# Finishing node batches inside the last six step groups of both graph convolutions

## The reference, cut to what matters

```python
def _gcn_layer(x, row, col, ew, W, b, n):
    deg = jax.ops.segment_sum(ew, col, num_segments=n)
    dis = jnp.where(deg > 0, jax.lax.rsqrt(jnp.maximum(deg, 1e-12)), 0.0)
    norm = dis[row] * ew * dis[col]
    h = x @ W
    msg = h[row] * norm[:, None]
    return jax.ops.segment_sum(msg, col, num_segments=n) + b
h = jax.nn.relu(_gcn_layer(x, row, col, ew, W1, b1, n))
out = _gcn_layer(h, row, col, ew, W2, b2, n)
x = _layernorm(x + out)
```

## Time and profile before

| | |
|---|---|
| median of three runs | 5566.82 us |
| lowest, highest | 5562.68, 5574.01 us |
| the profiled execution's own time | 5561.47 us |
| its span, first to last instruction | 5559.7 us |
| mean granted TensorE clock | 0.623 of full |
| GpSimd busy | 3855.6 us (69%) |
| VectorE busy | 3268.2 us (59%) |
| TensorE matmuls busy | 3136.6 us (56%) |
| ScalarE busy | 1490.0 us (27%) |

### The profile page before, as it was taken

One profiled execution on the slowest core, in us unless ns is written; L12 is line 12 of the kernel. 1 busy time (PEld: TensorE's weight loads), 2 busy tenths in 40 slices (PEclk: granted clock), 3 DMA queues, 4 the chain that ended last, 5 costly groups with the idle time before them and its releaser, 6 DMA issues. The chain is left out here.

```text
span 5559.7 us, 93044 instructions
## 1 busy us (share of the span) xinstructions
PE 3136.6 (56%) x16921; PEld 2725.2 (49%) x16922; DVE 3268.2 (59%) x11491; ACT 1490.0 (27%) x5614; POOL 3855.6 (69%) x4022
## 2 busy tenths in 40 slices
PE   4444444356666666679898989444444454444443
PEld 3333333345655555567777777333333343333332
DVE  6877777666777777754444444544444434444445
ACT  2333344336555555442222222300000010000001
POOL 3777777745777777637777775477777747777774
PEclk7555555568788788775555556655555565655555
DMA  5222222214444444312222221222222122222222
GB/s 124 54 53 53 53 53 57 47 46 127 131 131 131 131 131 131 101 44 58 53 54 53 57 53 30 56 55 55 54 53 53 52 59 55 55 55 54 53 53 58
DMA packets 229013, 386.29 MB, mean 69 GB/s; under 512 B 88799, under 2 KB 129084, under 8 KB 228688
## 3 DMA queue, kind: packets, MB, share of 16 engines
q0 software_dynamic: 141920, 294.25, 20.8%
q1 hardware_dynamic: 82924, 87.72, 5.3%
q10 hardware_dynamic: 3840, 0.99, 0.1%
HBM read 356.11 MB, written 26.56 MB: 69 GB/s over the span
## 5 line engine op out<-in xcount | busy, mean ns | idle before, releaser
L2298 POOL DMA_INDIRECT arena<-table_gcn,idx_now x1536 | 1457.9, 949 | 620.3 <-issue 418.8
L2393 PE MATMUL pair<-arena,hotf 128*128 x3328 | 752.9, 418 | 1111.9 <-POOLq L1881 1040.8
L2393 PEld LDWEIGHTS pair<-arena,hotf 128*128 128x128 f32 x3328 | 702.5, 320 | 1154.8 <-issue 1154.8
L2410 DVE TENSOR_SCALAR hotf<-iota,rel_now,ew_now 128x128 f32<-128x128 f32 x1664 | 444.1, 366 | 1000.7 <-PE pair L2396 925.9
L725 POOL DMA_INDIRECT arena<-table_attention,idx_now x832 | 813.0, 977 | 273.2 <-issue 208.1
L725 POOL DMA_INDIRECT arena<-table_key_value,idx_now x832 | 787.8, 947 | 276.0 <-issue 220.6
L1916 POOL DMA_INDIRECT arena<-table_edge_mlp,idx_now x784 | 754.1, 962 | 261.2 <-issue 210.9
L1132 PE MATMUL pair<-wide,hotf 128*128 128x130 f32 x1664 | 427.2, 436 | 645.2 <-ACT wide L1096 645.2
L1132 PEld LDWEIGHTS pair<-wide,hotf 128*128 128x128 f32 x1664 | 365.4, 323 | 709.7 <-ACT wide L1096 709.7
L2331 ACT COPY idx_now<-src_t 128x8 int32<-128x8 int32 x192 | 35.9, 197 | 1571.4 <-PE pair L2396 1209.7
L1468 PE MATMUL pair<-wide,hotf 128*128 128x132 f32 x1664 | 315.0, 348 | 232.8 <-DVE acc L1498 232.7
(11 more groups left out here) (384 smaller groups left out, 5666.3 us busy)
## 6 DMA issues: line engine op xcount, KB each, us to landing
arena<-table_gcn SPq DMA_DIRECT2D x1920, 0.5 KB
arena<-table_gcn ACTq DMA_DIRECT2D x1920, 0.5 KB
key<-rel_dram SPq DMA_DIRECT2D x104, 256.0 KB, 3.5
arena<-rel_dram SPq DMA_DIRECT2D x52, 512.0 KB
arena<-table_gcn,idx_now POOLq DMA_INDIRECT x1536
arena<-table_attention,idx_now POOLq DMA_INDIRECT x832, 2.5
arena<-table_key_value,idx_now POOLq DMA_INDIRECT x832, 2.9
arena<-table_edge_mlp,idx_now POOLq DMA_INDIRECT x784
```

The lines of the kernel that those rows point to most:

```text
L2298: q_.indirect_dma_start(conv_ring[:, slot * D:(slot + 1) * D], None, table, bass.IndirectOffsetOnAxis(ap=idx_now[:, slot:slot + 1].bitcast ...
L2393: t_.matmul(window[:, bass.ds(offset * D, D)], hot8[:, g % 2, u, :], conv_ring[:, bass.ds(slot * D, D)], start=False, stop=False)
L2410: last = v.tensor_scalar(out=hot8[:, g % 2, u, :], in0=iota[:, :], scalar1=rel_now[:, at], scalar2=ew_now[:, at], op0=ALU.is_equal, op1=AL ...
```

## The change

`convolution` gets four new arguments: what each engine does for settled batches. `SETTLED` is 98. Group k can only add to node tiles from 8k - 781 on, so once group 98 + j is added, batches 2j and 2j + 1 get no more sums. Behind each of groups 98 to 103 the engines run part j = k - 98 of the node work, and part 6 (batch 12) after the loop. Stages n4 and n5 as blocks of their own are gone.

In convolution one TensorE takes part too. From group 98 on it uses two sum windows instead of three (`pair[k % 2]`), and waits for one more clearing; the banks of `pair[2]` and `pair[3]` serve the node work, with one bank for `turn` and one for `hidden` instead of two each. The batches' temporaries move from `arena` and `hotf` into the unused `tab`.

```diff
+        SETTLED = -(-(ET - 1) // CG)
+        def convolution(name, table, table_out, settled_dve, settled_act, settled_sp, settled_pe=None, also_act=None, also_dve=None):
+            two_from = SETTLED if settled_pe else CSTEP_GROUPS
+            def window(k, g):
+                return pair[k % 2] if isinstance(k, int) and k >= two_from else pair[g % 3]
...
                         sp.sem_inc(sp_tile_in, 1)
+                    settled_sp(sp)
...
                         if k + AHEAD <= LONE * LONE_EVERY:
                             quarter(k + AHEAD)
+                        if k >= SETTLED:
+                            settled_act(act, k - SETTLED)
+                    for k in range(CSTEP_GROUPS - RING, CSTEP_GROUPS + 1):
+                        settled_act(act, k - SETTLED)
...
-                        pe.wait_ge(cleared, k + 1)
+                        pe.wait_ge(cleared, k + 2 if isinstance(k, int) and k >= two_from else k + 1)
...
                         last.then_inc(summed, 1)
+                        if settled_pe and isinstance(k, int) and k >= SETTLED:
+                            settled_pe(pe, k - SETTLED)
                     conv_rounds(pe, step, CSTEP_GROUPS)
+                    if settled_pe:
+                        settled_pe(pe, CSTEP_GROUPS - SETTLED)
...
-                        if not isinstance(k, int) or k + 3 < CSTEP_GROUPS:
+                        if not isinstance(k, int) or k + (3 if two_from > SETTLED else 2) < CSTEP_GROUPS:
...
                         back(k, g)
+                        if isinstance(k, int) and k >= SETTLED:
+                            dve.wait_ge(added, k + 1)
+                            settled_dve(dve, k - SETTLED)
...
                     conv_rounds(dve, both, CSTEP_GROUPS)
+                    settled_dve(dve, CSTEP_GROUPS - SETTLED)
```

More of the change, by code:

```diff
@@ new lines, in n4_pe, with turn, hidden, second @@
+        def n4_pe(pe, j):
+            def turn(b):
+                pe.wait_ge(n4_r, b + 1)
+                if b:
+                    pe.wait_ge(n4_rT_kept, b)
+                for u in range(BT):
+                    last = t_.transpose(turn_bank[:, u * P:(u + 1) * P], n4R[b % 4][:, u, :], ident[:, :])
+                last.then_inc(n4_rT, 1)
+            def hidden(b):
+                pe.wait_ge(n4_rT_kept, b + 1)
+                if b:
+                    pe.wait_ge(n4_h_kept, b)
+                t_.matmul(hidden_bank, wg1[:, :], n4T[b % 2], start=True, stop=True).then_inc(n4_h_mm, 1)
+            def second(b):
+                pe.wait_ge(n4_h_kept, b + 1)
+                if b >= 2:
+                    pe.wait_ge(n4_kept, b - 1)
+                for u in range(BT):
+                    at = slice(u * P, (u + 1) * P)
+                    last = t_.matmul(out_bank[b % 2][:, at], n4H[b % 2][:, at], wg2[:, :], start=True, stop=True)
+                last.then_inc(n4_mm, 1)
+            if j:
[7 more added lines that the diff above has]
+            hidden(2 * j)
+            if 2 * j + 1 == NB:
+                second(2 * j)
@@ new lines, in build, with n5_dve, sums, scales @@
+        n5_ch = Chain(v, n5_v)
+        def n5_dve(dve, j):
+            ch = n5_ch
+            def sums(b):
+                for t in range(b * BT, (b + 1) * BT):
+                    ch(v.scalar_tensor_tensor(out=xs[:, t, :], in0=acc[:, t, 0:D], scalar=dis[:, t:t + 1], in1=xs[:, t, :],
+                                              op0=ALU.mult, op1=ALU.add))
+                ch.wait()
+                for u in range(BT):
+                    ch(v.bn_stats(out=stat[:, u, 0:6], in_=xs[:, b * BT + u, :]))
+                ch.wait()
+                for u in range(BT):
+                    last = v.bn_aggr(out=n5M[b % 2][:, u, :], in_=stat[:, u, 0:6])
+                last.then_inc(n5_var, 1)
+            def scales(b):
+                f = n5F[b % 2]
+                dve.wait_ge(n5_std, b + 1)
+                ch(v.reciprocal(f[:, :, 0], f[:, :, 0]))
+                ch.wait()
+                v.scalar_tensor_tensor(out=f[:, :, 1], in0=n5M[b % 2][:, :, 0], scalar=-1.0, in1=f[:, :, 0],
+                                       op0=ALU.mult, op1=ALU.mult).then_inc(n5_factors, 1)
+            for b in (2 * j - 2, 2 * j - 1):
+                if b >= 0:
+                    scales(b)
+            for b in (2 * j, 2 * j + 1):
+                if b < NB:
+                    sums(b)
+            if 2 * j + 1 == NB:
+                scales(2 * j)
@@ new lines, in n5_act, with normalized, std @@
+        def n5_act(act, j):
+            def normalized(b):
+                act.wait_ge(n5_factors, b + 1)
+                for u in range(BT):
+                    t = b * BT + u
+                    last = s_.activation(xs[:, t, :], xs[:, t, :], ACT.Identity, scale=n5F[b % 2][:, u, 0:1], bias=n5F[b % 2][:, u, 1:2])
+                last.then_inc(n5_done, 1)
+            def std(b):
+                act.wait_ge(n5_var, b + 1)
+                if b >= 2:
+                    act.wait_ge(n5_done, b - 1)
+                s_.activation(n5F[b % 2][:, :, 0], n5M[b % 2][:, :, 1], ACT.Sqrt, bias=eps[:, 0:1]).then_inc(n5_std, 1)
+            for b in (2 * j - 2, 2 * j - 1):
+                if b >= 0:
+                    normalized(b)
+            for b in (2 * j, 2 * j + 1):
+                if b < NB:
+                    std(b)
+            if 2 * j + 1 == NB:
+                normalized(2 * j)
```

185 lines of the change are left out of this document (55 added, 130 removed).

## The result

The changed kernel's median was 5537.0 us (4 runs, 5527.95 to 5538.67) against 5569.7 us for the kernel before (4 runs): ratio 0.9939, 95% interval 0.9922 to 0.9956. Timed twice more, on other occasions, the ratio was 0.9966 (0.9952 to 0.9979) and 0.9953 (0.9940 to 0.9965). By medians that is a gain of 32.7, 21.2 and 26.5 us; the means of all 32 timings of before and 14 of the changed kernel are 25.7 us apart.

What follows compares the result with a forecast made beforehand. GpSimd's gathers were taken to pace the last groups, with about 72 us of n4 and n5 behind the convolutions. Gains of 21.2 (convolution two) and 3.4 (convolution one) make 24.6: 5566.82 to 5542.2 us, range 5532 to 5558.

Steps and rivals of the forecast that it cites:

- The step: Convolution two and n5: node work behind each group on VectorE and ScalarE; gain 21.7 us, 21.2 after output writes.
- the allowance: Convolution two: 13 output writes beside gathers might delay group 102; nothing to about 1 us, taken as 0.5.
- It fits, barely: Convolution two: VectorE's group work plus a part takes 9.8 us in a period of 10.05, so no backlog forms.
- The chain behind close 102: Convolution two: VectorE is the path from group 102's sum at 5515.32 to the last `normalized` ending at 5535.3.
- The ring: Convolution one's last groups: bound moves from GpSimd to VectorE, TensorE, VectorE; transposes start 5.33 us after the sum, cycle 13.0.
- The full-clock cycle: Convolution one: waiting 5.33, node work 3.27 and group 2.8 make a cycle of 11.4 us at full clock.
- The clock: Convolution one: TensorE's clock low at 5.33 us and up 4.0 us later in each cycle, making it 13.0 us.
- Full clock: Rival, convolution one: TensorE's clock stays full; gain there 10.0 us, 31.2 in all, 5535.6 us; chance 0.12.
- Half clock throughout: Rival, convolution one: clock stays down in all cycles, 15.3 us each; loss there 17.7, net gain 3.5, 5563.3 us; chance 0.10.
- Dear handovers, the slower case: Rival, convolution one: low clock, nine handovers costing 0.4 us more each, cycle 18.9; net 18.1 slower, 5584.9 us; chance 0.05.
- slip behind group 103: Rival: a wait makes VectorE's or ScalarE's parts run only after group 103; time stays at 5566.8 us; chance 0.03.
- Gathers slowed by VectorE: Rival, convolution two: busier VectorE holds up gathers, 2.3 us a period, 7.7 in all; gain 17, 5549.9 us; chance 0.06.

Runs made afterwards that it cites:

- changed_third: The changed kernel, unaltered, timed a third time against the kernel before: 5545.83 against 5572.37 us, ratio 0.9953.

## Why the prediction was right

**The total.** A gain of 24.6 us was forecast; the profiled pair shows 25.0, the stages 27 over three executions. 5537.0 lies in the range. That 24.6 and 25.0 agree so closely is luck: the stages gained 27.2 in that pair, and 2.2 were lost ahead of them by scatter. The first comparison's 32.7 us by medians is a draw of a program whose untouched part varies by 17 us.

**Convolution two.** The step held almost to the digit: 21.7 us before the allowance, 21.7 in the profiled pair (21.9 and 20.5 in the two others). "It fits, barely" was right: the 2.1 us between the end of part 3 and close 102 (5513.2 to 5515.32) were 2.5. The chain behind close 102 took 19.5 us for 20.0. The 0.5 us for output writes beside gathers was not seen: group 102 starts 3.1, 2.9 and 2.9 us after the last gather in the three executions, where it was 2.9.

**Convolution one.** The ring was named and it is what happened: transposes 5.24 us after the close for 5.33. Two terms were mis-sized and partly cancelled, which is luck too. The full-clock cycle is 12.0, not 11.4: from the first transpose to the end of `hidden` it takes 2.9 us for 3.27, but from there to the close 3.8 to 3.9 for 2.8, since the 0.3 us ahead of the opening and the 0.9 us ahead of the group's matmuls were left at almost nothing. The clock cost less than I took, because it was low for only 3.4 us in two of the four cycles and those took 12.0 and 12.1 us all the same: mean cycle 12.7 for 13.0. The cycle from close 102 to 103 took 8.9 for 8.5, the part behind close 103 12.8 us for 14.0, at full clock throughout. So the gain there was 5.6, not 3.4.

**The rivals.** Full clock: even forced from close 99 on, it gives 71.3 us from close 98, not 68. (Its sum kept the 0.8 us for a stretch at half clock.) Half clock throughout did not occur; the nearest to it was the first cycle, 12.5 of 13.4 us. Dear handovers, the slower case, came to 0.6 us per cycle, the gap ahead of the matmuls included, and not to 3.6. The parts did not slip behind group 103: part 3 of convolution two ended before close 102. Gathers slowed by VectorE was dismissed with one row, and that reading was too quick: the 0.946 of the earlier trace rows is a stretch in which nothing is held, while the first layer's gathers, in the same trace, had one of 1.870, and the convolutions' own line, L2298, one of 1.767. The lines' own views of the kernel before (shortest, median and longest in ns) would have told:

```profile
L725 POOL DMA_INDIRECT arena<-table_attention,idx_now x832: 940/944/1870, 103.2 to 1186.7; - x167
...
L2298 POOL DMA_INDIRECT arena<-table_gcn,idx_now x1536: 940/944/1767, 3533.7 to 5507.6; - x192
```

In convolution two one gather was held in one execution of three (`changed_third`, below), which cost it 1.2 us and not the rival's 7.7; in convolution one three were held each time, hidden behind the ring.

## What to carry to other kernels

Node work put behind a group is free on an engine that works ahead of the bound as long as it fits in the period (VectorE, two groups ahead, some 9.8 us of 10.05) and dear on one that stands in the chain (TensorE): there count the whole ring, from close to close, and put what others wait for first in the list. Here putting the add and the products ahead of the matrices, which nobody needed yet, gave 6 to 8 us, as much again as the change had gained in that stage. And an engine that is made busier beside a queue-bound one should be checked for single long instructions on that queue, by the maximum and not by the mean.

## What was not expected of the hardware

A gather on GpSimd takes 0.94 us. Two things that VectorE does made it longer in the tails.

The first is the pair of L2489 products (tensor_tensor, two SBUF inputs, 1.27 us). Every pair beside which a gather ran held one: 25 in the eight executions that have them. The gather took 1.3 to 2.3 us and ended 0.21 or 0.22 us after the pair, whether it had begun in the memset ahead of the pair or in the pair itself.

The second is a step from the memset straight to another kind of 128x128 operation that reads SBUF, while a gather is running. With tensor_scalar products behind the memset the gather ended 0.88 us after the memset did, in 11 of 12 cases (the twelfth had begun so late that it took its plain 0.94); with the x_nodes operations 0.99 or 1.00 us after, in all 6. So it is the longer the earlier it began: up to 1.86 and 2.02 us. One from `changed_third`:

```profile
5479.28 1.98 POOL L2307 DMA_INDIRECT arena<-table_gcn,idx_now  x1 [0.30 <-issue]
5479.35 0.91 DVE L2441 MEMSET pair<- 128x1024 f32 x1 [0.29 <-DVE acc L2438]
5480.17 1.05 DVE L2584 SCALAR_TENSOR_TENSOR x_nodes<-acc,dis,x_nodes 128x128 f32<-128x128 f32 x4
```

In the first execution of the changed kernel no gather was running at that step. The next one began 0.14 us after the memset's end, beside the same operations, and took its 0.94 us:

```profile
5474.48 0.91 DVE L2441 MEMSET pair<- 128x1024 f32 x1 [0.29 <-DVE acc L2438]
5475.30 1.08 DVE L2584 SCALAR_TENSOR_TENSOR x_nodes<-acc,dis,x_nodes 128x128 f32<-128x128 f32 x4
5475.53 0.94 POOL L2307 DMA_INDIRECT arena<-table_gcn,idx_now  x1 [0.30 <-issue]
```

So in the tails the moment at which the gather begins decides. A hold that spans the end of the memset ended 1.40 us after it with the tensor_tensor pair and 0.88 with tensor_scalar products, so the form saves 0.5 us of it. That is read from the traces; no run set the moment. Nor is it the whole rule: behind the memset and a reciprocal of 128x4 none of 8 gathers was held, and in the loop ahead of the tails (from 4000 us on, 13 executions), with the matrices straight behind the memset, 24 of 67 gathers ended 0.88 us after it and 43 took their 0.94.

The Trainium skill (SBUF — State Buffer, "Who interferes with whom") describes a lock between VectorE operations with two SBUF inputs and GpSimd operations that read SBUF, one waiting for the whole of the other. The holds to the end of L2489 agree with such a lock, and its inference that descriptor making is spared does not hold for these gathers. The section also counts tensor_scalar among the operations that can take the shared ports, in their two-port modes; no run here shows in which mode the products ran. The holds that begin in the memset, and the many two-input operations that hold nothing (the earlier trace rows and the fence above), are not explained by it.
